# First attention: more of the softmax weights turned by DMA and VectorE, fewer by TensorE, with new step orders

## The chip, the core and the metric

The kernel runs on one core of a Trainium2 chip. The metric is the device time in microseconds (us) of one execution, lower is better. The engines are TensorE (PE, with its weight loads as PEld), VectorE (DVE), ScalarE (ACT), GpSimd (POOL) and SyncE (SP, which here only issues DMAs).

## What is computed

Two layers, each an attention onto a context and a feed-forward part, on x of shape (4, 256, 512) and a context of shape (4, 1601, 512), all in fp32. The change is in the first attention alone:

```python
# latents = layernorm(x): (4, 256, 512); context: (4, 1601, 512)
N_HEADS, N_KV_HEADS, HEAD_DIM = 32, 4, 128
hidden = concatenate([context, latents], axis=1)              # 1857 keys a batch
q = (latents @ Wq).reshape(b, 256, 4, 8, 128)
k = (hidden @ Wk).reshape(b, 1857, 4, 128)
v = (hidden @ Wv).reshape(b, 1857, 4, 128)
scores = einsum('bqhgd,bkhd->bhgqk', q, k) / sqrt(128)
attn = softmax(scores, axis=-1)
out = einsum('bhgqk,bkhd->bqhgd', attn, v).reshape(b, 256, 4096)
x = x + out @ Wo
...
```

The rest (a gated expert block, a second attention and a routed expert block) is untouched.

## The kernel before

`grouped_attention_block` first projects queries, keys and values (`split_projections`), which go to DRAM as pairs of fp32r numbers, a high and a low part. Each product of two such pairs is three matmuls, high by high, high by low, low by high (`three`). Then come 128 units, one for each of 4 batches and 32 heads; a unit has 256 tokens as two tiles j = 0, 1 of 128 rows (`QT` = 2).

For a unit and a tile j, TensorE makes the scores of 128 tokens by 1857 keys in four PSUM banks `ps_s`: half 0 is banks 0 and 1 (1024 keys), half 1 is banks 2 and 3 (833 keys), with a call of `scores(u, j, half)` each. VectorE takes the maximum of each half (`maximum`) and the negated, scaled maximum of the row (`negate_maximum`). ScalarE takes the exponential of each half into `probs` (`exponentials`), with its sum read by a second small instruction. The four banks are all there are: `scores(u, j, half)` waits until the exponential of the same half of the tile before it is done.

For the product with v the weights must be transposed, keys on the partitions. Two ways are in use:

- The first 1024 keys (`TURNED`, four runs of `RUN` = 256) are *traded*: for each tile SP issues four DMAs (`trade`), each moving one run of all 128 rows of `probs` onto 32 partitions of `traded`, which lies in the idle tile `xn`. Then VectorE's 32x32 transpose (`turn_traded`, line 898) gives a pair of key blocks for all 256 tokens in `turned`, ScalarE copies it to fp32r (`turned_high`, line 836), GpSimd subtracts to get the low part (`low`, line 707), and TensorE weighs it with v (`weigh_turned`, six matmuls of 256 columns). Four such pairs a unit, in rings of four.
- The last 833 keys are transposed by TensorE (`turn_plain`, line 752, fourteen transposes a unit into `ps_x`), copied by ScalarE (`plain_high`, line 845), subtracted by VectorE (`plain_low`, line 908) and weighed (`weigh_plain`): four pairs, of which the last has one tile of 65 keys.

All engines run over the units in steps (`run`), each engine with its own `step`, in which the calls for several units are written out by hand in the order in which the engine issues them: u, v, w, l, z are the units r, r-1, r-2, r-3, r-4. Nothing else sets the order; engines meet at semaphores (`probs_done`, `neg_max_done`, `turn_done`, `t_hi_done`, `t_done`, `x_hi_done`, `x_done` and so on), and a wait stands in the queue of its engine ahead of what follows it. SP's queue holds the trades, the loads of the next keys, values (`piece`) and queries, and the stores of the outputs (`store_output`, after VectorE's `take_output`).

After the units, `output_projection_block` multiplies with Wo.

Of the kernel before, what the change touches and what calls it, by code (L numbers as in the profile page):

```python
# [6 lines left out]
F32 = mybir.dt.float32  # L7
# [4 lines left out]
P = 128  # L12
# [476 lines left out]
def grouped_attention_block(nc, held, x, ctx_in, wq, wk, wv, wo, x_res, xn, stats, ident, ones):  # L489
# [21 lines left out]
    RUN = 256  # L511
# [5 lines left out]
    PPAIRS = -(-PLAIN // 2)  # L517
    BLOCKS = TBLOCKS + PLAIN
    plain_rows = lambda m: P if m < PLAIN - 1 else REST
    pair_tiles = lambda e: range(2 * e, min(2 * e + 2, PLAIN))  # L520
    RING, PRING, XBANKS = 4, 4, 2
    KPIECES = 4
    VPLAIN = (PLAIN - 1) // 2
# [3 lines left out]
    assert QT == 2 and len(CHUNKS) == 4 and HPG == 8 and TURNED <= 2 * BANK and TBLOCKS % 2 == 0 and WIDTH % 2 == 0  # L527
    assert PLAIN % 2 == 1 and TPAIRS * HEADS % RING == 0 and PPAIRS * HEADS % XBANKS == 0 and PPAIRS * HEADS % PRING == 0

    with ExitStack() as ctx:  # L530
# [16 lines left out]
        with ExitStack() as stack:  # L547
# [12 lines left out]
            def load_values(sp, b, g, a, c):  # L560
# [4 lines left out]
                elif c < RUNS + 2:  # L565
                    lo, hi = [(0, VPLAIN), (VPLAIN, PLAIN - 1)][c - RUNS]
                    sp.dma_start(v_buf[a][:, TBLOCKS + lo:TBLOCKS + hi, :].bitcast(F32),
                                 keys_of[TURNED + P * lo:TURNED + P * hi, g, :].rearrange("(m i) d -> i m d", i=P)
                                 ).then_inc(v_loaded[a], 16)
                else:  # L570
                    sp.dma_start(v_buf[a][0:REST, BLOCKS - 1, :].bitcast(F32), keys_of[KEYS - REST:KEYS, g, :]).then_inc(v_loaded[a], 16)
# [17 lines left out]
            traded = xn[:, :, :].rearrange("p t d -> p (t d)")[:, 0:2 * QT * TURNED].rearrange("p (a j g r) -> p a j g r", a=2, j=QT, g=RUNS)  # L589
            turned = sb("turned", [P, RING, 2, TOK])  # L590
            t_hi, t_lo = sb("t_hi", [P, RING, 2, TOK], F32R), sb("t_lo", [P, RING, 2, TOK], F32R)
            x_hi, x_lo = sb("x_hi", [P, PRING, 2, TOK], F32R), sb("x_lo", [P, PRING, 2, TOK], F32R)
# [45 lines left out]
            def _(sp):  # L638
                def trade(u, j):
                    if not u.live:  # L640
                        return
                    sp.wait_ge(probs_done, 4 * u.n + 2 * j + 1)
                    if j == 0:
                        wait(sp, turn_done, TPAIRS * (u.n - 1))
                    for c in range(RUNS):
                        sp.dma_start(traded[SQ * c:SQ * (c + 1), u.a, j, :, :], probs[j][u.a][:, RUN * c:RUN * (c + 1)]
                                     ).then_inc(trade_done[j][u.a], 16)
# [11 lines left out]
                def piece(u):  # L659
# [7 lines left out]
                    else:  # L667
                        if i == KPIECES:
                            wait(sp, tv_ps, TPAIRS * (u.n - KPIECES - HPG))
                            wait(sp, xv_ps, PPAIRS * (u.n - KPIECES - HPG))  # L670
# [31 lines left out]
            def _(pool):  # L702
                def low(u, p):
                    if u.live:
                        slot = (TPAIRS * u.r + p) % RING
                        pool.wait_ge(t_hi_done, TPAIRS * u.n + p + 1)
                        pool.tensor_tensor(t_lo[:, slot, :, :], turned[:, slot, :, :], t_hi[:, slot, :, :].bitcast(F32), ALU.subtract  # L707
                                           ).then_inc(t_done, 1)
# [11 lines left out]
            def _(pe):  # L720
# [20 lines left out]
                def turn_plain(u, e):  # L741
                    if not u.live:
                        return
                    bank = (PPAIRS * u.r + e) % XBANKS
                    if e == 0:
                        pe.wait_ge(probs_done, 4 * (u.n + 1))
                    wait(pe, x_done, PPAIRS * u.n + e + 1 - XBANKS)
                    for m in pair_tiles(e):
                        rows, c0 = plain_rows(m), TURNED + P * m
                        for j in range(QT):  # L750
                            col = TOK * (m % 2) + P * j
                            tr = pe.transpose(ps_x[0:rows, bank, col:col + P], probs[j][u.a][:, c0:c0 + rows], turn[:, :])  # L752
                    tr.then_inc(x_ps, 1)

                def output_free(u):
# [1556 lines left out]
```

## Time and profile before

| | |
|---|---|
| median of 2 runs | 3322.86 us |
| lowest, highest | 3320.5, 3325.22 us |
| span of the profiled execution | 3324.5 us, between the two runs, so that nothing stands beside the span |
| PE, DVE, ACT, POOL busy | 3185.9 (96%), 2156.2 (65%), 1702.5 (51%), 872.7 (26%) us |
| first attention's units | from some 540 to 2119 us |
| DMA queue of SP | 51.1% of 16 engines' span, 449.22 MB |

A busy share is the union of an engine's instructions over the span. Matmuls are pipelined, and their shown durations overlap, so their pace is read from one start to the next. Times in rows are us unless marked ns. In rows by order of time the first number is the start, the second the duration, and "x4" says that four instructions in a row were merged; what stands in brackets at the end is the idle time ahead and what ended it.

### The profile page before, as it was taken

The numbers are of one execution on the slowest core, as the hardware profiler recorded it, in microseconds if no ns is written. First come the engines' busy times: TensorE is split into PE (matmuls) and PEld (weight loads), VectorE is DVE, ScalarE is ACT, GpSimd is POOL, SyncE is SP. The second block draws the span as 40 slices with busy tenths as digits, with TensorE's granted clock in tenths as the row PEclk, the third lists the DMA queues.
The fourth block names the chain that finished last, engine by engine and source line by source line (L and its number), as shares of the span: only waits on it lengthen the run. The fifth ranks groups of instructions, "written<-read, shape, count | busy, mean of one in ns | idle before, by whom it ended". The sixth has DMA issues, their size and how long they took to land. (4 is left out here: it accounts for less than half of the span.)

```text
span 3324.5 us, 55156 instructions
## 1 busy us (share of the span) xinstructions
PE 3185.9 (96%) x18912; PEld 2815.0 (85%) x18912; DVE 2156.2 (65%) x3275; ACT 1702.5 (51%) x3206; POOL 872.7 (26%) x703
## 2 busy tenths in 40 slices
PE   8999998999999999999999999898988989889999
PEld 8898886999999998999989999786778878868887
DVE  4333334888888887888878888544555667745555
ACT  3332344666666666667666666323425445532222
POOL 0000121444444443444444444321003223400000
PEclk9999998999999999999999999999998999989999
DMA  7665785777766766776667775574201101111111
GB/s 251 217 210 193 241 269 167 160 161 163 164 159 161 160 160 152 162 159 160 159 153 161 160 161 125 161 238 164 73 31 38 30 26 36 39 39 47 46 39 44
DMA packets 360308, 452.24 MB, mean 136 GB/s; under 512 B 32316, under 2 KB 289644, under 8 KB 360072
## 3 DMA queue, kind: packets, MB, share of 16 engines
q1 hardware_dynamic: 360072, 449.22, 51.1%
q8 instruction: 133, 2.18, 0.3%
q14 instruction: 103, 0.84, 0.1%
HBM read 201.45 MB, written 113.43 MB: 95 GB/s over the span
## 5 line engine op out<-in xcount | busy, mean ns | idle before, releaser
L707 POOL TENSOR_TENSOR a_t_lo<-a_turned,a_t_hi 128x512 fp32r<-128x512 f32 x512 | 649.8, 1291 | 939.8 <-ACT a_t_hi L836 939.8
L827 ACT ACTIVATE a_probs<-a_ps_s,a_neg_max 128x1024 f32<-128x1024 f32 (+1 forms) x512 | 529.5, 1034 | 476.0 <-DVE a_neg_max L879 470.1
L872 DVE TENSOR_REDUCE a_half_max<-a_ps_s 128x1 f32<-128x1024 f32 (+1 forms) x512 | 571.2, 1116 | 189.5 <-PE a_ps_s L724 185.3
L722 PE MATMUL a_ps_s<-a_k_buf,a_q_buf 128*128 128x512 f32 (+1 forms) x1024 | 419.7, 410 | 18.2 <-ACT a_probs L827 11.9
L723 PE MATMUL a_ps_s<-a_k_buf,a_q_buf 128*128 128x512 f32 (+1 forms) x1024 | 386.1, 377 | 0.0
L724 PE MATMUL a_ps_s<-a_k_buf,a_q_buf 128*128 128x512 f32 (+1 forms) x1024 | 385.3, 376 | 0.0
L908 DVE TENSOR_TENSOR a_x_lo<-a_ps_x,a_x_hi 128x512 fp32r<-128x512 f32 (+1 forms) x512 | 314.5, 614 | 107.8 <-ACT a_x_hi L845 107.8
L454 DVE TENSOR_TENSOR p_out<-p_ps_j,p_out 128x512 fp32r<-128x512 f32 (+3 forms) x196 | 153.0, 781 | 326.6 <-ACT p_out L383 326.6
L898 DVE STREAM_TRANSPOSE a_turned<-xn 128x512 f32<-128x512 f32 x512 | 357.8, 699 | 1.6 <-POOL a_t_lo L707 1.6
L383 ACT ACTIVATE p_out<-p_ps_j 128x512 fp32r<-128x512 f32 (+3 forms) x196 | 141.9, 724 | 339.8 <-PE p_ps_j L288 339.7
L722 PE MATMUL a_ps_o<-a_t_hi,a_v_buf 128*128 128x256 f32 x1024 | 298.8, 292 | 6.2 <-issue 3.6
L836 ACT ACTIVATE a_t_hi<-a_turned 128x512 fp32r<-128x512 f32 x512 | 298.4, 629 | 2.0 <-DVE a_turned L898 2.0
L723 PE MATMUL a_ps_o<-a_t_lo,a_v_buf 128*128 128x256 f32 x1024 | 287.5, 281 | 0.0
L724 PE MATMUL a_ps_o<-a_t_hi,a_v_buf 128*128 128x256 f32 x1024 | 287.4, 281 | 0.0
L845 ACT ACTIVATE a_x_hi<-a_ps_x 128x512 fp32r<-128x512 f32 (+1 forms) x512 | 274.5, 537 | 24.6 <-PE a_ps_x L752 13.2
L752 PE MATMUL a_ps_x<-a_turn,a_probs 128*128 128x128 f32 (+1 forms) x1792 | 279.0, 272 | 0.0
L722 PE MATMUL a_ps_o<-a_x_hi,a_v_buf 128*128 128x256 f32 (+1 forms) x896 | 262.4, 293 | 0.0
L724 PE MATMUL a_ps_o<-a_x_hi,a_v_buf 128*128 128x256 f32 (+1 forms) x896 | 251.6, 281 | 0.0
L723 PE MATMUL a_ps_o<-a_x_lo,a_v_buf 128*128 128x256 f32 (+1 forms) x896 | 251.4, 281 | 0.0
L752 PEld LDWEIGHTS a_ps_x<-a_turn,a_probs 128*128 128x128 f32 (+1 forms) x1792 | 219.1, 140 | 35.0 <-issue 0.2
L722 PEld LDWEIGHTS a_ps_s<-a_k_buf,a_q_buf 128*128 128x128 f32 x1024 | 195.0, 190 | 49.6 <-issue 11.7
L724 PEld LDWEIGHTS a_ps_s<-a_k_buf,a_q_buf 128*128 128x128 f32 x1024 | 194.5, 190 | 34.2
(319 smaller groups left out, 7389.7 us busy)
## 6 DMA issues: line engine op xcount, KB each, us to landing
xn<-a_probs SPq DMA_DIRECT2D x1024, 128.0 KB, 3.4
a_q_all<-p_out SPq DMA_DIRECT2D x64, 512.0 KB
a_q_buf<-a_q_all SPq DMA_DIRECT2D x128, 256.0 KB, 3.3
a_k_buf<-a_k_all SPq DMA_DIRECT2D x64, 464.5 KB, 4.0
a_v_all<-p_out SPq DMA_DIRECT2D x56, 512.0 KB
a_k_all<-p_out SPq DMA_DIRECT2D x48, 384.0 KB
a_v_buf<-a_v_all SPq DMA_DIRECT2D x64, 256.0 KB
a_o_all<-a_o_part SPq DMA_DIRECT2D x128, 128.0 KB, 3.0
```

Source lines behind the costliest of these rows:

```text
L454: dve.tensor_tensor(job_views(n, 1)[0], ps, hi.bitcast(F32), ALU.subtract).then_inc(job_done, 1)
L707: pool.tensor_tensor(t_lo[:, slot, :, :], turned[:, slot, :, :], t_hi[:, slot, :, :].bitcast(F32), ALU.subtract).then_inc(t_done, 1)
L722: pe.matmul(o, w_hi, m_hi, start=first, stop=False)
L723: pe.matmul(o, w_hi, m_lo, start=False, stop=False)
L724: return pe.matmul(o, w_lo, m_hi, start=False, stop=last)
L752: tr = pe.transpose(ps_x[0:rows, bank, col:col + P], probs[j][u.a][:, c0:c0 + rows], turn[:, :])
L827: act.activation(probs[j][u.a][:, lo:hi], s_flat[:, lo:hi], ACT.Exp, bias=neg_max[:, j:j + 1], scale=SCALE, accum_out=half_sum[:, bass.ds( ...
L836: act.activation(t_hi[:, slot, :, :], turned[:, slot, :, :], ACT.Copy).then_inc(t_hi_done, 1)
L845: act.activation(x_hi[0:rows, slot, 0:m, :], ps_x[0:rows, bank, 0:TOK * m].rearrange("p (m n) -> p m n", m=m), ACT.Copy).then_inc(x_hi_don ...
L872: dve.reduce_max(half_max[:, half:half + 1], s_flat[:, lo:hi], AX.X).then_inc(max_done, 1)
L898: dve.transpose(turned[:, slot, :, :].rearrange("p k (q r) -> p k q r", r=SQ), traded[:, u.a, :, :, 2 * SQ * p:2 * SQ * (p + 1)].rearrange ...
L908: dve.tensor_tensor(x_lo[0:rows, slot, 0:m, :], ps_x[0:rows, bank, 0:TOK * m].rearrange("p (m n) -> p m n", m=m), x_hi[0:rows, slot, 0:m, ...
```

## The change

`RUN` goes from 256 to 448: 1792 of 1857 keys are traded, in seven pairs a unit where there were four, and each DMA of a trade moves 224 KB where it moved 128 KB. TensorE transposes the last 65 keys only, two transposes a unit; `turn_plain`, `plain_high`, `plain_low` and `weigh_plain` are called once a unit. `traded` gets a tile of its own beside `xn` for odd units. `turned` keeps its ring of four pairs; `t_hi` and `t_lo` get seven places. `trade` waits for the first half of the exponentials ahead of runs 0 and 1 and for the second ahead of runs 2 and 3. Values are loaded in five pieces. The orders in the step functions are new: a step of SP stores an output between the two trades, and those of GpSimd, TensorE, ScalarE and VectorE are rewritten throughout.

```diff
-    RUN = 256
+    RUN = 448
...
-    RING, PRING, XBANKS = 4, 4, 2
+    RING, PRING, XBANKS = 4, 2, 2
+    EARLY = 3
...
-    VALUE_PIECES = [(0, 1), (2, 3), (4,), (5, 6)]
+    VALUE_PIECES = [(0,), (1,), (2,), (3, 4)]
...
-            t_hi, t_lo = sb("t_hi", [P, RING, 2, TOK], F32R), sb("t_lo", [P, RING, 2, TOK], F32R)
+            t_hi, t_lo = sb("t_hi", [P, TPAIRS, 2, TOK], F32R), sb("t_lo", [P, TPAIRS, 2, TOK], F32R)
...
                 def trade(u, j):
...
-                    sp.wait_ge(probs_done, 4 * u.n + 2 * j + 1)
...
                     for c in range(RUNS):
+                        if c % 2 == 0:
+                            sp.wait_ge(probs_done, 4 * u.n + 2 * j + c // 2 + 1)
...
                     trade(u, 0)
                     piece(Unit(b, r + HPG))
+                    store_output(Unit(b, r - 3))
                     trade(u, 1)
-                    store_output(Unit(b, r - 3))
                     queries(Unit(b, r + 2))
...
             @block.gpsimd
                 def step(b, r):
                     w, l = Unit(b, r - 2), Unit(b, r - 3)
-                    low(l, 1)
-                    low(l, 2)
-                    low(l, 3)
-                    low(w, 0)
+                    for p in range(EARLY, TPAIRS):
+                        low(l, p)
+                    for p in range(EARLY):
+                        low(w, p)
...
             @block.tensor
                 def step(b, r):
-                    weigh_turned(z, 2)
-                    weigh_plain(z, 2)
-                    turn_plain(l, 1)
-                    weigh_plain(z, 3)
+                    weigh_turned(l, 0)
                     scores(v, 0, 0)
-                    turn_plain(l, 2)
+                    weigh_turned(l, 1)
+                    weigh_plain(l)
                     scores(v, 0, 1)
-                    weigh_turned(z, 3, last=True)
-                    turn_plain(l, 3)
-                    weigh_turned(l, 0, first=True)
-                    weigh_plain(l, 0)
-                    weigh_turned(l, 1)
+                    weigh_turned(l, 2)
+                    weigh_turned(l, 3)
+                    turn_plain(w)
                     scores(v, 1, 0)
-                    turn_plain(w, 0)
+                    weigh_turned(l, 4)
                     scores(v, 1, 1)
-                    weigh_plain(l, 1)
+                    weigh_turned(l, 5)
+                    weigh_turned(l, 6)
...
             @block.scalar
                 def step(b, r):
-                    exponentials(v, 1, 0)
-                    plain_high(w, 1)
-                    exponentials(v, 1, 1)
+                    exponentials(w, 1, 0)
+                    turned_high(l, 3)
+                    exponentials(w, 1, 1)
+                    turned_high(l, 4)
+                    exponentials(v, 0, 0)
+                    turned_high(l, 5)
+                    turned_high(l, 6)
+                    exponentials(v, 0, 1)
+                    plain_high(w)
                     turned_high(w, 0)
                     turned_high(w, 1)
-                    plain_high(w, 2)
-                    exponentials(u, 0, 0)
-                    plain_high(w, 3)
-                    exponentials(u, 0, 1)
                     turned_high(w, 2)
-                    turned_high(w, 3)
-                    plain_high(v, 0)
...
             @block.vector
                 def step(b, r):
-                    plain_low(l, 1)
-                    turn_traded(l, 1)
+                    turn_traded(l, 3)
+                    turn_traded(l, 4)
                     maximum(v, 0, 0)
+                    take_output(z)
+                    turn_traded(l, 5)
                     maximum(v, 0, 1)
                     negate_maximum(v, 0)
-                    turn_traded(l, 2)
-                    take_output(z)
-                    plain_low(l, 2)
-                    turn_traded(l, 3)
+                    turn_traded(l, 6)
+                    plain_low(w)
                     maximum(v, 1, 0)
-                    plain_low(l, 3)
+                    turn_traded(w, 0)
                     maximum(v, 1, 1)
                     negate_maximum(v, 1)
-                    plain_low(w, 0)
-                    turn_traded(w, 0)
+                    turn_traded(w, 1)
+                    turn_traded(w, 2)
```

## Rows read from the trace of the kernel before

**Rows 1.** Busy time by stretch, 700 to 1700 us: PE, PEld, DVE, ACT, POOL, clock, DMA.
```profile
700.00:1700.00 1000.00, 995.32 (x6844) 917.38 (x6843) 808.59 (x1237) 686.94 (x1318) 418.75 (x330) 1.00 0.71 160
```

**Rows 2.** The tile of the maxima: count, duration (ns) least, median, most, first and last start.
```profile
L879 DVE TENSOR_SCALAR a_neg_max<-a_half_max x256: 214/214/217, 550.0 to 2098.1; 128x1 f32<-128x1 f32 x128
```

**Rows 3.** In order of time, PE, from 1000 to 1013 us.
```profile
1004.01 0.42 PE L722 MATMUL a_ps_s<-a_k_buf,a_q_buf 128*128 128x512 f32 x1
...
1005.43 0.60 PE L752 MATMUL a_ps_x<-a_turn,a_probs 128*128 128x128 f32 x4
1005.79 0.48 PE L722 MATMUL a_ps_s<-a_k_buf,a_q_buf 128*128 128x512 f32 x1
...
1007.02 0.28 PE L722 MATMUL a_ps_o<-a_t_hi,a_v_buf 128*128 128x256 f32 x1
...
1007.74 0.38 PE L752 MATMUL a_ps_x<-a_turn,a_probs 128*65 128x128 f32 x2
...
1010.13 0.50 PE L722 MATMUL a_ps_s<-a_k_buf,a_q_buf 128*128 128x512 f32 x1
```

**Rows 4.** In order of time, DVE, from 1000 to 1026 us.
```profile
1001.27 1.03 DVE L872 TENSOR_REDUCE a_half_max<-a_ps_s 128x1 f32<-128x833 f32 x1
1002.33 0.21 DVE L879 TENSOR_SCALAR a_neg_max<-a_half_max 128x1 f32<-128x1 f32 x1
...
1005.17 0.70 DVE L898 STREAM_TRANSPOSE a_turned<-xn 128x512 f32<-128x512 f32 x1
1005.79 1.19 DVE L872 TENSOR_REDUCE a_half_max<-a_ps_s 128x1 f32<-128x1024 f32 x1
1007.22 1.03 DVE L872 TENSOR_REDUCE a_half_max<-a_ps_s 128x1 f32<-128x833 f32 x1 [0.24 <-PE a_ps_s L724]
1008.37 0.21 DVE L879 TENSOR_SCALAR a_neg_max<-a_half_max 128x1 f32<-128x1 f32 x1
1008.50 0.70 DVE L898 STREAM_TRANSPOSE a_turned<-xn 128x512 f32<-128x512 f32 x1
```

**Rows 5.** In order of time, ACT, from 1000 to 1026 us.
```profile
1002.67 1.12 ACT L827 ACTIVATE a_probs<-a_ps_s,a_neg_max 128x1024 f32<-128x1024 f32 x1 [1.88 <-DVE a_neg_max L879]
...
1008.87 1.11 ACT L827 ACTIVATE a_probs<-a_ps_s,a_neg_max 128x1024 f32<-128x1024 f32 x1 [1.85 <-DVE a_neg_max L879]
1009.88 0.19 ACT L827 ACTIVATION_READ_ACCUMULATOR a_probs<-a_ps_s,a_neg_max  x1
1009.98 0.37 ACT L845 ACTIVATE a_x_hi<-a_ps_x 65x256 fp32r<-65x256 f32 x1
1010.24 0.95 ACT L827 ACTIVATE a_probs<-a_ps_s,a_neg_max 128x833 f32<-128x833 f32 x1
...
1011.17 1.15 ACT L836 ACTIVATE a_t_hi<-a_turned 128x512 fp32r<-128x512 f32 x2
1012.33 0.60 ACT L845 ACTIVATE a_x_hi<-a_ps_x 128x512 fp32r<-128x512 f32 x1
```

**Rows 6.** Groups by line and shape, 700 to 1700 us: busy us, mean ns, idle before.
```profile
L707 POOL TENSOR_TENSOR a_t_lo<-a_turned,a_t_hi 128x512 fp32r<-128x512 f32 x330 | 418.9, 1291 | 579.8 <-ACT a_t_hi L836 579.8
...
L908 DVE TENSOR_TENSOR a_x_lo<-a_ps_x,a_x_hi 65x256 fp32r<-65x256 f32 x83 | 34.0, 410 | 0.0
```

**Rows 7.** DMA issues on the page: count, KB each, median us from issue to landing.
```profile
xn<-a_probs SPq DMA_DIRECT2D x1024, 128.0 KB, 3.4
```

**Rows 8.** PE in order of time, at the stage's start and its end.
```profile
551.48 0.51 PE L722 MATMUL a_ps_s<-a_k_buf,a_q_buf 128*128 128x512 f32 x1 [2.60 <-ACT a_probs L827]
...
2103.18 0.36 PE L722 MATMUL a_ps_o<-a_t_hi,a_v_buf 128*128 128x256 f32 x1 [1.74 <-POOL a_t_lo L707]
```

**Rows 9.** Busy time by stretch, as in the first group, at the same two places.
```profile
545.00:550.00 5.00, 3.87 (x11) 2.86 (x10) 2.28 (x3) 0.24 (x1) 0.00 (x0) 0.66 0.02 5
...
2102.00:2104.00 2.00, 0.82 (x7) 0.85 (x8) 1.72 (x5) 1.51 (x4) 2.00 (x2) 1.00 1.07 161
```

More of the change, by code:

```diff
@@ L669, in piece @@
                             wait(sp, tv_ps, TPAIRS * (u.n - KPIECES - HPG))
-                            wait(sp, xv_ps, PPAIRS * (u.n - KPIECES - HPG))
+                            wait(sp, xv_ps, u.n - KPIECES - HPG)
                         for c in VALUE_PIECES[i - KPIECES]:
@@ L739, in scores, with turn_plain, weigh_turned @@
                     mm.then_inc(s_ps, 1)
-                def turn_plain(u, e):
+                def turn_plain(u):
                     if not u.live:
                         return
[L744 to L752, printed above, removed]
-                    tr.then_inc(x_ps, 1)
-                def output_free(u):
-                    wait(pe, copy_done, u.n - 1)
-                    if u.first_of_group:
-                        pe.wait_ge(v_loaded[u.group_a], 16 * VPIECES * (u.group_use + 1))
-                def weigh_turned(u, p, first=False, last=False):
+                    bank = u.r % XBANKS
+                    pe.wait_ge(probs_done, 4 * (u.n + 1))
+                    wait(pe, x_done, u.n + 1 - XBANKS)
+                    for j in range(QT):
+                        tr = pe.transpose(ps_x[0:REST, bank, P * j:P * j + P], probs[j][u.a][:, TURNED:KEYS], turn[:, :])
+                    tr.then_inc(x_ps, 1)
+                def weigh_turned(u, p):
                     if not u.live:
                         return
-                    v, slot = v_buf[u.group_a], (TPAIRS * u.r + p) % RING
-                    if first:
-                        output_free(u)
+                    v = v_buf[u.group_a]
+                    if p == 0:
+                        wait(pe, copy_done, u.n - 1)
+                        if u.first_of_group:
+                            pe.wait_ge(v_loaded[u.group_a], 16 * VPIECES * (u.group_use + 1))
                     pe.wait_ge(t_done, TPAIRS * u.n + p + 1)
@@ L768, in weigh_turned, with weigh_plain @@
                         k = 2 * p + i
[L769 to L770 removed]
+                        mm = three(ps_o[:, u.a, 0:TOK], v[:, k, 0:HD], v[:, k, HD:2 * HD], t_hi[:, p, i, :], t_lo[:, p, i, :],
+                                   k == 0, k == TBLOCKS - 1)
                     mm.then_inc(tv_ps, 1)
[L773 removed]
+                def weigh_plain(u):
                     if not u.live:
                         return
[L776 to L784 removed]
+                    v, slot = v_buf[u.group_a], u.r % PRING
+                    pe.wait_ge(x_done, u.n + 1)
+                    three(ps_o[:, u.a, 0:TOK], v[0:REST, TBLOCKS, 0:HD], v[0:REST, TBLOCKS, HD:2 * HD], x_hi[0:REST, slot, :],
+                          x_lo[0:REST, slot, :], False, False).then_inc(xv_ps, 1)
                 def turn_sums():
@@ L824, in exponentials @@
                         wait(act, trade_done[j][u.a], TRADE * u.use)
-                        wait(act, x_ps, PPAIRS * (u.n - 1))
+                        wait(act, x_ps, u.n - 1)
                     lo, hi = HALVES[half]
```

67 lines of the change are left out of this document (21 added, 46 removed).

## The prediction

> **What bounds the kernel now.** I read the busy times by stretch first. From 700 to 1700 us, the middle of the first attention, TensorE is busy for 995 of 1000 us at a granted clock of 1.00, VectorE for 809, ScalarE for 687, GpSimd for 419, and the DMA engines for 0.71 [rows 1]. Taken alone this says: TensorE is the bound, so fewer transposes there is time won. It has to be checked against the order of the work, because the change also rewrites that order.
>
> The first and the last negated maximum stand 1548.1 us apart [rows 2], and there are 127.5 units between them: 12.14 us a unit, half a unit 6.07. I then followed one half unit in order of time, to see whether anything beside TensorE's own work closes in the same time. It does. The reader should follow the four score banks: scores(j,0) starts; 1.42 us later come four transposes (0.36), then scores(j,1) (1.23 with the switch back) [rows 3]; 0.20 after the last score the second maximum starts, 1.15 later the negation, 0.50 later the exponential [rows 4, 5], whose sum is read 1.20 after its start, and 0.06 after that the next scores(j,0) starts, since it overwrites the first two banks. Sum 6.12 us, which is just the distance of the two score starts in the rows (1004.01 to 1010.13). So today two limits meet: the loop through the score banks, and TensorE's queue, which fills the 3.1 us between scores(j,1) and the next scores(j,0) with weighing. Whatever is now put *into* that loop costs its full length; what is taken from TensorE outside of it gives nothing.
>
> **The change, part by part.** Write n for the unit whose scores are made.
>
> *TensorE's work.* Twelve of fourteen transposes a unit go: three groups of four, 0.36 us each and some 0.07 for the switch back (scores(j,1) took 1.23; its columns at the pace of scores(j,0), 1.42 for six of 512, would take 1.16) [rows 3]: 3 x 0.43 = 1.3 us. The weighing keeps its size (45 matmuls of 256 columns, 0.72 for six). TensorE alone would need 12.1 - 1.3 = 10.8 us a unit.
>
> *VectorE, ScalarE, GpSimd.* Three full subtractions (plain_low) become three more 32x32 transposes (turn_traded, one each 0.62 us [rows 4]); one subtraction of 65x256, 0.41 us, stays [rows 6]. ScalarE trades copies for copies of the same shape. GpSimd goes from four to seven subtractions of 1.29 us: 9.0 us a unit [rows 6]. None of these sums reaches 12 us, so no engine's load is the bound; the order is.
>
> *The order.* All of these queues work in the order in which the step functions issue, so I wrote out who stands in front of whom. Three places matter.
>
> (1) ScalarE: `turned_high(w, 1)` and `turned_high(w, 2)` end a step, and `exponentials(w, 1, 0)` of the next step stands behind them. VectorE makes what they read, `turn_traded(w, 1)` and `turn_traded(w, 2)`, only *after* `negate_maximum(v, 1)`. So the exponential that was ready 0.34 to 0.50 after the negation now waits for two transposes and a copy more.
>
> (2) VectorE: `plain_low(w)` stands ahead of both `maximum(v, 1, ...)`. It needs `plain_high(w)`, which on ScalarE stands behind `exponentials(v, 0, 1)` and two turned_high. So the maxima of the second half wait for nearly all of ScalarE's step.
>
> (3) TensorE: between scores(v,0,0) and scores(v,0,1) stand a weigh_turned and the plain weighing, 0.72 + 0.36, where four transposes stood.
>
> The cycle that this closes, from exponentials(n,0,0) once round to exponentials(n+1,0,0), worked out from rows already shown [rows 3 to 5]:
>
> First half: the exponential until ScalarE's next instruction 1.11 (1008.87 to 1009.98); two turned_high 1.16; exponential of 833 until the next instruction 0.93; plain_high of 65x256 0.37, and 0.06 to another engine; plain_low 0.41; first maximum 1.19; turn_traded(n-1,0) 0.62; second maximum until its negation 1.10 (1.06 and 1.15 in the rows); negation until the next transpose 0.13; two transposes 0.62 + 0.70, and 0.06; turned_high 0.58. Sum 9.04 us.
>
> Second half: exponentials(n,1,0) until its sum is read, and over to TensorE, 1.26; scores(n+1,0,0) 1.42; weigh_turned 0.72; plain weighing 0.36; scores(n+1,0,1) 1.16; to the start of the maximum 0.20; maximum 1.10; negation to exponential 0.42. Sum 6.64 us.
>
> Together 15.68 us. VectorE's rows start up to 0.08 before the one ahead has ended (1005.17 plus 0.70 against 1005.79), twice in this chain, so I take 15.5. The low end is 15.2 (both maxima at 1.06, the negation's hand-over at 0.34, the copy's overlap). For the high end, no row shows a turned_high waiting right behind its transpose or a plain_low behind so late a copy; if each of some nine crossings costs 0.12 instead of 0.06 or a little less, it is 16.2. Below 15.2 I see nothing, since each link is an instruction in a queue or a wait that the code names.
>
> Each of the queues was assumed to keep its order. The rows bear that out: VectorE, ScalarE and GpSimd never start an instruction ahead of one that stands before it in the step [rows 4, 5]. The Trainium skill says it outright, on the page "TensorE: Matmul & The Clock Gate", section "Architectural detail: the array is 16× 32×32, not 1× 128×128": only TensorE's queue may pull something forward, and then only weight loads, while ScalarE's and VectorE's are strict first-in first-out. By that rule, too, the exponential cannot pass the turned_high ahead of it.
>
> *Beside the cycle.* TensorE would work 10.8 of 15.5 us, in pieces, with gaps of up to 1.8 us (behind weigh_turned(l,6), until GpSimd has made the next unit's first pair, and again until scores). GpSimd's 9.0 us lie inside the 15.5. The ring of four turned pairs doesn't bind: turn_traded(w,2) needs low(l,5), done over 4 us before.
>
> *DMA.* A trade grows from 128 KB to 224 KB in the same number of pieces. Today a unit costs 0.71 x 12.1 = 8.6 us of all DMA engines [rows 1], for 1.9 MB, of which the eight trades are 1.05 MB. If a piece costs the same whatever its length it stays 8.6; if by bytes, 8.6 + 0.75 x 4.7 = 12.1 us. Both are under 15.5. Latency: the last trade of a unit's second half is issued about 4 us after its exponential starts and lands 3.4 us after that [rows 7], or 6 us if it grows with the bytes, thus at 7.4 to 10; turn_traded(w,0) wants it at 6.6 + 5.2 = 11.8. Hidden, by 2 us at least. SP's two waits instead of one per trade and the moved store_output hold up only SP, whose eight trades of 0.6 us each leave it idle for over half of the unit.
>
> *The sum.* 127.5 x (15.5 - 12.14) = 428 us. Start-up and tail stay: their first units run on the score loop alone, as now, and the last unit has three more pairs to go through GpSimd, 4 us. The profiled execution spans 3324.5 us, 1.6 us off the median 3322.9. So 3324.5 + 428 = about 3750 us; by the ends of the cycle 3715 and 3842.
>
> **The rivals.** *Faster: TensorE stays the bound.* If ScalarE did not stand still at the end of its step, and the weighing filled each gap, a unit would take 10.8 us: 3324.5 - 127.5 x 1.3 = 3158 us. For it: TensorE's 995 of 1000 us. Against it: the two named waits lie in program order, and the score loop alone, with 1.08 and 0.72 us put between its halves, is longer than 10.8. It decides the other way only if turn_traded(w,1) and (w,2) were ready before the negation, which VectorE's order excludes. Chance 0.06.
>
> *Only the score loop grows.* If places (1) and (2) were covered, what is left is 6.64 plus a second half of 6.64 - 0.36 = 6.28: 12.9 us a unit, 3421 us (12.6 us, 3383, with the shorter hand-overs). Chance 0.06.
>
> *TensorE's clock falls.* With gaps, the granted clock can drop to the lower of its two levels. In the start of this stage it was 0.66 where gaps of 2.6 us lay between the bursts; near its end it stayed at 1.00 with a gap of 1.74 us and TensorE busy 0.82 of 2 us [rows 8, 9]. My longest gap is 1.8, so I expect 1.00. At the lower level throughout, TensorE's links in the cycle (1.42 + 0.72 + 0.36 + 1.16 = 3.66 us) double: 3750 + 467 = 4217, but its whole work would then be 21 us a unit, without the gaps that brought the clock down, so about half the time at most: some 3985 us. [...] Chance 0.08.
>
> **How the numbers follow.** The cycle as worked out: 0.80, with 3750 us. Its ends are 3715 and 3842; with start-up and tail uncertain by some ten us I give 3700 to 3850. The other cases, 0.20 together, stay outside. About 2% (66 us) is what a measurement of this kernel can tell from no change: faster 0.06; within 2% 0.03, half of the second rival; slower 0.91.
>
> **What would show it.** Units of about 15.5 us between negated maxima; TensorE busy about 0.7 in the stage, at a clock of 1.00; VectorE idle some 3 us a unit ahead of plain_low, waiting for ScalarE's x_hi; ScalarE waiting for VectorE's turned at the end of its step, and no longer for the negated maximum ahead of half of its exponentials; TensorE waiting for the exponentials. It would be wrong if the exponentials of the second half still start 0.4 us after their negation, if VectorE waits for traded data ahead of turn_traded(w,0), or if the clock is under 1.

## The result, and the profile after

The changed kernel took 3909.4 us (median of two runs, 3908.3 and 3910.5), against 3322.9 before: a ratio of 1.177, with an interval of 1.174 to 1.179. It is slower, as forecast, but the time lies above the range of 3700 to 3850. The page of the changed kernel: its span, the busy time of each engine, the granted clock and the DMA share in 40 slices, and the two kinds of trade (count, KB each, us from issue to landing):

```profile
span 3908.7 us, 53700 instructions
...
PE 3268.7 (84%) x17376; PEld 2806.6 (72%) x17376; DVE 2146.6 (55%) x3275; ACT 1707.4 (44%) x3206; POOL 1348.7 (35%) x1087
...
PEclk9999989999998999899898989988989899999999
DMA  7665979999999999999999999997741111111111
...
xn<-a_probs SPq DMA_DIRECT2D x512, 224.0 KB, 5.9
a_traded<-a_probs SPq DMA_DIRECT2D x512, 224.0 KB, 5.9
```

The tile of the negated maxima, which answers to [rows 2]:

```profile
L855 DVE TENSOR_SCALAR a_neg_max<-a_half_max x256: 212/214/216, 550.5 to 2681.4; 128x1 f32<-128x1 f32 x128
```

2681.4 - 550.5 is 2130.9 us, over 127.5 units 16.71 us a unit, where it was 12.14. The difference, 4.57 us, times 127.5 is 583 us; the spans differ by 3908.7 - 3324.5 = 584. So all of the loss lies inside the stage, as 4.57 us a unit on average; start and tail did not move.

Busy time by stretch (PE, PEld, DVE, ACT, POOL, granted clock, DMA share, GB/s), first the middle of the stage, which answers to [rows 1], then stretches that are read below:

```profile
700.00:2400.00 1700.00, 1290.06 (x7195) 1121.20 (x7194) 987.22 (x1523) 849.22 (x1623) 892.54 (x711) 0.91 1.04 162
...
1262.00:1264.00 2.00, 0.86 (x4) 0.60 (x3) 0.60 (x2) 2.00 (x5) 2.00 (x2) 0.64 1.00 245
1264.00:1266.00 2.00, 2.00 (x6) 1.55 (x5) 0.00 (x0) 1.23 (x3) 2.00 (x3) 0.50 1.00 221
1266.00:1268.00 2.00, 2.00 (x11) 1.96 (x10) 1.73 (x3) 0.00 (x0) 0.64 (x1) 0.50 1.07 154
1268.00:1270.00 2.00, 2.00 (x10) 1.71 (x10) 0.50 (x2) 0.00 (x0) 0.00 (x0) 0.65 1.06 153
...
1236.00:1262.00 26.00, 19.23 (x124) 16.88 (x123) 16.67 (x27) 13.50 (x26) 12.98 (x11) 1.00 1.04 162
```

No engine is full any more: TensorE is busy 0.76 of the stage instead of 0.995, VectorE 0.58, GpSimd 0.53, ScalarE 0.50. Two columns are not as forecast: the clock is 0.91, and the DMA share is 1.04 (the share adds up the time of all packets, so packets that overlap can bring it over 1). Who waits for whom, in the same stretch (engine, line, waited for: us in total, times, longest):

```profile
POOL a_t_lo L701 <- ACT a_t_hi L815: 807.5, 309, 6.8
DVE a_half_max L848 <- PE a_ps_s L718: 376.0, 177, 3.7
ACT a_t_hi L815 <- DVE a_turned L874: 351.8, 204, 2.7
DVE a_x_lo L882 <- ACT a_x_hi L822: 305.6, 101, 3.4
ACT a_probs L806 <- DVE a_neg_max L855: 288.3, 61, 6.2
...
PE a_ps_s L716 <- ACT a_probs L806: 237.3, 203, 1.8
...
DVE a_turned L874 <- DMA xn<-a_probs: 0.3, 1, 0.3
```

Some 102 units lie in these 1700 us. VectorE's plain_low (a_x_lo) waits 101 times for ScalarE's copy, about 3 us each: place (2) of the prediction. ScalarE's turned_high waits 204 times, twice a unit, for VectorE's transposes. In the unit shown next the first of the two waits, 2.32 us, is for `turn_traded(w, 0)`, which VectorE makes between the two maxima that place (2) holds up; the second, 1.15 us, is the one of place (1). Only one wait for traded data is there, of 0.3 us.

ScalarE in order of time (start, us, instruction, and in brackets the idle time ahead of it and what ended it), which answers to [rows 5]; one unit, then the three exponentials that bound the halves of a later one:

```profile
1204.28 1.11 ACT L806 ACTIVATE a_probs<-a_ps_s,a_neg_max 128x1024 f32<-128x1024 f32 x1 [5.15 <-PE a_ps_x L742]
...
1207.35 0.37 ACT L822 ACTIVATE a_x_hi<-a_ps_x 65x256 fp32r<-65x256 f32 x1
1210.04 0.63 ACT L815 ACTIVATE a_t_hi<-a_turned 128x512 fp32r<-128x512 f32 x1 [2.32 <-DVE a_turned L874]
1211.82 1.23 ACT L815 ACTIVATE a_t_hi<-a_turned 128x512 fp32r<-128x512 f32 x2 [1.15 <-DVE a_turned L874]
1212.95 1.09 ACT L806 ACTIVATE a_probs<-a_ps_s,a_neg_max 128x1024 f32<-128x1024 f32 x1
...
1221.13 1.11 ACT L806 ACTIVATE a_probs<-a_ps_s,a_neg_max 128x1024 f32<-128x1024 f32 x1 [5.02 <-DVE a_neg_max L855]
...
1238.09 1.11 ACT L806 ACTIVATE a_probs<-a_ps_s,a_neg_max 128x1024 f32<-128x1024 f32 x1 [5.14 <-PE a_ps_x L742]
...
1246.76 1.10 ACT L806 ACTIVATE a_probs<-a_ps_s,a_neg_max 128x1024 f32<-128x1024 f32 x1
...
1253.40 1.11 ACT L806 ACTIVATE a_probs<-a_ps_s,a_neg_max 128x1024 f32<-128x1024 f32 x1 [3.48 <-DVE a_neg_max L855]
```

VectorE in the first of these units, which answers to [rows 4]:

```profile
1207.76 0.42 DVE L882 TENSOR_TENSOR a_x_lo<-a_ps_x,a_x_hi 65x256 fp32r<-65x256 f32 x1 [3.12 <-ACT a_x_hi L822]
1208.10 1.21 DVE L848 TENSOR_REDUCE a_half_max<-a_ps_s 128x1 f32<-128x1024 f32 x1
...
1210.87 0.21 DVE L855 TENSOR_SCALAR a_neg_max<-a_half_max 128x1 f32<-128x1 f32 x1
1211.00 2.48 DVE L874 STREAM_TRANSPOSE a_turned<-a_traded 128x512 f32<-128x512 f32 x4
```

The negated maximum of the second half is there at 1211.08. Its exponential starts at 1212.95, behind two copies that wait for the transposes that VectorE begins at 1211.00. Ahead of that, the maximum at 1208.10 stands behind plain_low, which has stood still for 3.12 us. From exponential to exponential, the first half is 1212.95 - 1204.28 = 8.67 us (worked out: 9.04), the second 1221.13 - 1212.95 = 8.18 (worked out: 6.64). In the later unit, from 1238.09 to 1253.40, the first half takes 8.67 us again and the second 6.64, just as worked out.

So the excess is in the second half, that of TensorE's links, and only in some units. TensorE in order of time, two units, of which the first is the later one of ScalarE's rows; the scores of a unit begin at 1239.35, 1254.66 and 1272.84:

```profile
1239.35 0.50 PE L716 MATMUL a_ps_s<-a_k_buf,a_q_buf 128*128 128x512 f32 x1 [1.29 <-ACT a_probs L806]
...
1245.88 0.38 PE L716 MATMUL a_ps_o<-a_t_hi,a_v_buf 128*128 128x256 f32 x1 [1.58 <-POOL a_t_lo L701]
...
1248.00 0.50 PE L716 MATMUL a_ps_s<-a_k_buf,a_q_buf 128*128 128x512 f32 x1 [1.16 <-ACT a_probs L806]
...
1254.66 0.50 PE L716 MATMUL a_ps_s<-a_k_buf,a_q_buf 128*128 128x512 f32 x1 [1.15 <-ACT a_probs L806]
1255.00 0.40 PE L717 MATMUL a_ps_s<-a_k_buf,a_q_buf 128*128 128x512 f32 x1
1255.24 0.40 PE L718 MATMUL a_ps_s<-a_k_buf,a_q_buf 128*128 128x512 f32 x1
...
1261.19 0.39 PE L716 MATMUL a_ps_o<-a_t_hi,a_v_buf 128*128 128x256 f32 x1 [1.59 <-POOL a_t_lo L701]
...
1263.31 0.80 PE L716 MATMUL a_ps_s<-a_k_buf,a_q_buf 128*128 128x512 f32 x1 [1.14 <-ACT a_probs L806]
1263.90 0.63 PE L717 MATMUL a_ps_s<-a_k_buf,a_q_buf 128*128 128x512 f32 x1
1264.33 0.63 PE L718 MATMUL a_ps_s<-a_k_buf,a_q_buf 128*128 128x512 f32 x1
...
1272.84 0.50 PE L716 MATMUL a_ps_s<-a_k_buf,a_q_buf 128*128 128x512 f32 x1 [1.28 <-ACT a_probs L806]
```

The first unit is 15.31 us long and runs wholly at a clock of 1.00 (the stretch from 1236 to 1262 above). The second is 18.18 us long: from 1263.31 on its scores follow each other every 0.43 us, where those from 1255.00 took 0.24, while the clock is 0.50 from 1264 to 1268 and 0.64 and 0.65 in the stretches beside them: some 7 us at the low level, worked out from these four shares. The longest gap of either unit is 1.59 us. At the mean of 16.71, the clock costs 16.71 - 15.31 = 1.40 us a unit, 178 us in all, if 15.31 stands for every unit at full clock; the first experiment tests that.

### The profile page after: what moved, and what is told of

The parts are those of the page before. It is cut to its first block and busy times, and to the rows that moved or that the text cites. A ratio compares the mean times of both kernels' runs of the same rounds, so it can differ in the third digit from the quotient of the medians.

```text
span 3908.7 us, 53700 instructions
## 1 busy us (share of the span) xinstructions
PE 3268.7 (84%) x17376; PEld 2806.6 (72%) x17376; DVE 2146.6 (55%) x3275; ACT 1707.4 (44%) x3206; POOL 1348.7 (35%) x1087
## 5 line engine op out<-in xcount | busy, mean ns | idle before, releaser
L701 POOL TENSOR_TENSOR a_t_lo<-a_turned,a_t_hi 128x512 fp32r<-128x512 f32 x896 | 1126.2, 1281 | 1051.0 <-ACT a_t_hi L815 1051.0
L815 ACT ACTIVATE a_t_hi<-a_turned 128x512 fp32r<-128x512 f32 x896 | 542.3, 625 | 448.8 <-DVE a_turned L874 448.8
L716 PE MATMUL a_ps_o<-a_t_hi,a_v_buf 128*128 128x256 f32 x1792 | 542.4, 303 | 217.2 <-POOL a_t_lo L701 204.8
L716 PE MATMUL a_ps_s<-a_k_buf,a_q_buf 128*128 128x512 f32 (+1 forms) x1024 | 452.2, 442 | 306.7 <-ACT a_probs L806 300.8
L716 PEld LDWEIGHTS a_ps_o<-a_t_hi,a_v_buf 128*128 128x128 f32 x1792 | 366.0, 204 | 260.6 <-POOL a_t_lo L701 177.0
L717 PE MATMUL a_ps_o<-a_t_lo,a_v_buf 128*128 128x256 f32 x1792 | 526.5, 294 | 0.0
L718 PE MATMUL a_ps_o<-a_t_hi,a_v_buf 128*128 128x256 f32 x1792 | 523.4, 292 | 0.0
L716 PEld LDWEIGHTS a_ps_s<-a_k_buf,a_q_buf 128*128 128x128 f32 x1024 | 215.1, 210 | 391.4 <-ACT a_probs L806 313.9
L718 PE MATMUL a_ps_s<-a_k_buf,a_q_buf 128*128 128x512 f32 (+1 forms) x1024 | 432.5, 422 | 0.0
L717 PE MATMUL a_ps_s<-a_k_buf,a_q_buf 128*128 128x512 f32 (+1 forms) x1024 | 428.7, 419 | 0.0
L717 PEld LDWEIGHTS a_ps_o<-a_t_lo,a_v_buf 128*128 128x128 f32 x1792 | 365.0, 204 | 16.3
L718 PEld LDWEIGHTS a_ps_o<-a_t_hi,a_v_buf 128*128 128x128 f32 x1792 | 361.8, 202 | 0.0
L874 DVE STREAM_TRANSPOSE a_turned<-a_traded 128x512 f32<-128x512 f32 x448 | 293.3, 687 | 18.2 <-issue 13.7
L874 DVE STREAM_TRANSPOSE a_turned<-xn 128x512 f32<-128x512 f32 x448 | 293.3, 687 | 1.1 <-POOL a_t_lo L701 0.5
L718 PEld LDWEIGHTS a_ps_s<-a_k_buf,a_q_buf 128*128 128x128 f32 x1024 | 219.9, 215 | 43.4
L717 PEld LDWEIGHTS a_ps_s<-a_k_buf,a_q_buf 128*128 128x128 f32 x1024 | 218.3, 213 | 28.3
```

What stands on the lines that cost most here:

```text
L701: pool.tensor_tensor(t_lo[:, p, :, :], turned[:, slot, :, :], t_hi[:, p, :, :].bitcast(F32), ALU.subtract).then_inc(t_done, 1)
L716: pe.matmul(o, w_hi, m_hi, start=first, stop=False)
L717: pe.matmul(o, w_hi, m_lo, start=False, stop=False)
L718: return pe.matmul(o, w_lo, m_hi, start=False, stop=last)
L815: act.activation(t_hi[:, p, :, :], turned[:, slot, :, :], ACT.Copy).then_inc(t_hi_done, 1)
L874: dve.transpose(turned[:, slot, :, :].rearrange("p k (q r) -> p k q r", r=SQ), traded[u.a][:, :, :, 2 * SQ * p:2 * SQ * (p + 1)].rearrange ...
```

## The experiments

Theory A: the order of the queues makes the cycle of 15.3 us, and the low clock of TensorE adds 1.4 us. The rivals: B, the DMA engines, whose share reads 1.04, make the rest (or all) of it; C, the sum of 15.5 was right by accident, and moving the two places gives nothing. Times below are medians; the time of a unit, the clock, the share, GB/s and the rows are of the one profiled execution, which lies up to 29 us from its median.

**TensorE kept busy.** Fourteen matmuls a unit that nobody reads are put where it waits; nothing is taken away:

```diff
+                def fill(count, bank):
+                    for _ in range(count):
+                        pe.matmul(ps_x[:, bank, TOK:TOK + P], turn[:, :], turn[:, :], start=True, stop=True)
...
+                    fill(6, r % XBANKS)
                     weigh_turned(l, 0)
+                    fill(4, r % XBANKS)
                     scores(v, 0, 0)
...
                     turn_plain(w)
+                    fill(4, (r + 1) % XBANKS)
                     scores(v, 1, 0)
```

> The changed kernel with 14 matmuls of 128x128 a unit added on TensorE, in the three places where it stands still (ahead of the first weighing pair, ahead of scores(v,0,0), ahead of scores(v,1,0)); they write a free part of a ps_x bank that nobody reads, so the output is the same. Theory: the cycle of queue orders is 15.3 us a unit at a clock of 1.00 (1239.35 to 1254.66 in the changed kernel's trace), and the clock, 0.90 in the stage, adds the other 1.4 us. Then the added work lifts the clock to 1.00 and the kernel gets FASTER: 3324.5 + 127.5 x (15.3 - 12.14) = 3727 us, 3710 to 3760. Rival, DMA sets the pace (share 1.04): no change, 3909. Rival, the gaps are not what lowers the clock: 3909 or more, up to 14 x 0.2 us x 128 = 358 us more if the added matmuls lie on the path.

Measured: 3765.0 us, 1.134 times before (1.132 to 1.136), so 144 us faster than the changed kernel with more work, and 5 us above the range that was expected. The negated maxima run from 555.1 to 2527.4: 15.47 us a unit. The stage as a stretch:

```profile
700.00:2300.00 1600.00, 1503.34 (x10217) 1363.90 (x10218) 1003.99 (x1548) 865.93 (x1656) 913.00 (x725) 1.00 1.07 176
```

And TensorE in order of time:

```profile
1202.61 0.39 PE L716 MATMUL a_ps_o<-a_t_hi,a_v_buf 128*128 128x256 f32 x1 [0.26 <-POOL a_t_lo L701]
...
1204.73 0.50 PE L716 MATMUL a_ps_s<-a_k_buf,a_q_buf 128*128 128x512 f32 x1 [0.25 <-ACT a_probs L813]
```

Where gaps of 1.58 and 1.16 us lay, 0.26 and 0.25 are left, the clock is 1.00 throughout, and the unit has the forecast length. The trades are as large as in the changed kernel, at a share of 1.07. The clock was the excess.

**Half of each trade.** From the third unit on, only half of each run is moved, so that half of the turned weights are stale:

```diff
-                        sp.dma_start(traded[u.a][SQ * c:SQ * (c + 1), j, :, :], probs[j][u.a][:, RUN * c:RUN * (c + 1)]
+                        m = RUN if u.n < 2 else RUN // 2
+                        sp.dma_start(traded[u.a][SQ * c:SQ * (c + 1), j, :, 0:m], probs[j][u.a][:, RUN * c:RUN * c + m]
```

> The changed kernel, but from the third unit on each trade moves only the first half of each run, 112 KB instead of 224; the other half of the traded tile keeps old weights, so the attention is computed from partly stale weights. Same number of DMAs, same semaphores. Theory (order of the queues and the clock): no change, 3909 within 1%, landing times fall from 5.9 us. Rival, DMA sets the pace: a unit's 2.7 MB falls to 1.8 MB, the period from 16.7 to some 12 to 15 us, so 3300 to 3700 us.

Measured: 3898.4 us, 1.173 (1.171 to 1.175): 0.3% off the changed kernel, 16.66 us a unit, the clock still at 0.91:

```profile
700.00:2300.00 1600.00, 1217.12 (x6789) 1058.44 (x6790) 930.92 (x1437) 801.30 (x1533) 842.30 (x671) 0.91 0.38 108
```

A trade lands after 2.7 us instead of 5.9, the share falls from 1.04 to 0.38, and the time stays. With the single wait of 0.3 us above, rival B is out for the changed kernel: its transfers are hidden.

**Place (1) undone.** On ScalarE the copies of pairs 1 and 2 move behind the exponential that they stood ahead of:

```diff
                     exponentials(w, 1, 0)
-                    turned_high(l, 3)
+                    turned_high(l, 1)
                     exponentials(w, 1, 1)
+                    turned_high(l, 2)
+                    turned_high(l, 3)
                     turned_high(l, 4)
...
                     turned_high(w, 0)
-                    turned_high(w, 1)
-                    turned_high(w, 2)
```

> The changed kernel with ScalarE's order alone changed: turned_high(w,1) and (w,2) no longer stand ahead of the next exponentials(w,1,0), but behind it. Theory: two transposes, a copy and their hand-overs (2.5 us) leave the cycle for a hand-over of 0.42, and weigh_turned(l,1) comes 0.4 later: 15.3 - 1.7 = 13.6 to 14.4 us a unit at full clock, 3510 to 3613 us; if the clock falls as often as now, up to 3790. Rival, DMA sets the pace: 3909.

Measured: 3682.7 us, 1.108 (1.104 to 1.113), 14.85 us a unit. ScalarE in order of time:

```profile
1203.72 1.11 ACT L806 ACTIVATE a_probs<-a_ps_s,a_neg_max 128x1024 f32<-128x1024 f32 x1 [2.94 <-DVE a_neg_max L855]
...
1209.71 0.63 ACT L815 ACTIVATE a_t_hi<-a_turned 128x512 fp32r<-128x512 f32 x1 [2.54 <-DVE a_turned L874]
1210.88 1.11 ACT L806 ACTIVATE a_probs<-a_ps_s,a_neg_max 128x1024 f32<-128x1024 f32 x1 [0.54 <-DVE a_neg_max L855]
```

The exponential now waits for its negation alone, and the first half is 7.16 us instead of 8.67. The time lies above the range expected at full clock (3510 to 3613) and inside the one with the clock still falling: it was 0.96 from 700 to 2300 us. Rival C is out.

**Places (1) and (2) undone,** with whole and with half trades. On VectorE `plain_low(w)` moves behind the negated maximum and `turn_traded(w, 1)`; the fifth kernel has the half trades of the second one as well:

```diff
                     turn_traded(l, 6)
-                    plain_low(w)
                     maximum(v, 1, 0)
...
                     turn_traded(w, 1)
+                    plain_low(w)
                     turn_traded(w, 2)
```

> As the run before it, and on VectorE plain_low(w) is moved from ahead of the maxima of the second half to behind the negation and one transpose. Theory: both detours are out, the score loop and the 0.4 of weigh_turned(l,1) are left: 6.28 + 7.05 = 13.3 us a unit, 12.6 if the loop's hand-overs are short, 3385 to 3480 us, clock near 1.00. Rival, DMA sets the pace at 16.7 us: 3909, with VectorE's turn_traded waiting for the traded tile.

> The kernel with ScalarE's and VectorE's detours both taken out, with half the bytes in each trade from the third unit on (so partly stale weights). It measured 14.7 us a unit with full trades where 12.6 to 13.3 was worked out. If the trades' bytes are the difference: 12.6 to 13.5 us a unit, 3385 to 3500 us, clock 1.00, no wait for a traded tile. If something in the queues was overlooked: 3640 as before.

Measured: 3640.9 us, 1.096 (1.092 to 1.099), 14.69 us a unit with whole trades, hardly better than place (1) alone and a miss, since 3385 to 3480 us was expected; with half trades 3494.4 us, 1.051 (1.049 to 1.053), 13.50 a unit. The stage with whole trades:

```profile
700.00:2300.00 1600.00, 1274.47 (x7675) 1108.66 (x7673) 1062.21 (x1623) 897.15 (x1732) 961.03 (x757) 0.96 1.07 184
```

And with half trades:

```profile
700.00:2000.00 1300.00, 1099.59 (x6827) 948.21 (x6826) 945.91 (x1442) 798.43 (x1539) 856.30 (x674) 0.99 0.47 133
```

Here the size of a trade matters, by 1.2 us a unit, where it was worth 0.05 in the changed kernel. The first of the two has waits for traded data (46.3 us in 29 waits for one buffer, 18.5 in 16 for the other, in 1300 us), the second has none. These waits come to 0.7 of the 1.2 us; how much of the rest is the clock, 0.96 against 0.99, was not separated. The bound that places (1) and (2) had hidden is the next one: the trades. Place (2) was undone only together with place (1), and place (3) only in the rewrite that follows, so neither has a price of its own.

**The score loop freed of everything.** All step orders are rewritten so that both halves of the scores stand next to each other and the weighing fills the wait for the exponentials. The new orders, with the loops written out (GpSimd, left out here, now takes four pairs early instead of three):

```diff
# TensorE
+ scores(v, 0, 0); scores(v, 0, 1)
+ weigh_plain(z); weigh_turned(z, 4); weigh_turned(z, 5); weigh_turned(z, 6); turn_plain(w)
+ scores(v, 1, 0); scores(v, 1, 1)
+ weigh_turned(l, 0); weigh_turned(l, 1); weigh_turned(l, 2); weigh_turned(l, 3)
# ScalarE
+ exponentials(v, 0, 0); exponentials(v, 0, 1); turned_high(l, 4); turned_high(l, 5); turned_high(l, 6); plain_high(w)
+ exponentials(v, 1, 0); exponentials(v, 1, 1); turned_high(w, 0); turned_high(w, 1); turned_high(w, 2); turned_high(w, 3)
# VectorE
+ maximum(v, 0, 0); maximum(v, 0, 1); negate_maximum(v, 0)
+ turn_traded(l, 4); turn_traded(l, 5); turn_traded(l, 6); take_output(z); plain_low(l)
+ maximum(v, 1, 0); maximum(v, 1, 1); negate_maximum(v, 1)
+ turn_traded(w, 0); turn_traded(w, 1); turn_traded(w, 2); turn_traded(w, 3)
```

> All step orders written anew around the score loop, with the 448 runs kept: TensorE makes both halves of a tile's scores one behind the other and weighs in the gap behind them (four pairs, then three and the plain block); ScalarE and VectorE do the copies and transposes in the gap behind each tile's exponentials and negation; the plain subtraction comes a step later. If only the order matters, a half unit is 1.26 + 1.42 + 1.16 + 0.20 + 1.10 + 0.42 = 5.56 us: 11.2 us a unit, 3205 us. What the order of two rows back showed speaks for a second limit: there VectorE waited for traded tiles, at 14.7 us a unit and a DMA share of 1.07. If the trades cannot go faster than that, this run is no faster: 14.7 us, 3650 us.

And the same with half trades, half of the turned weights stale:

> The kernel with both halves of the scores together, but from the third unit on each trade moves the first half of each run only (112 KB), so the attention uses partly stale weights. Theory (order gives 11.2 us a unit as soon as the trades are out of the way): 3180 to 3240 us. Rival (it is not the trades' bytes that hold the run with full trades): the same time as that run.

Measured: with whole trades 3412.8 us, 1.027 (1.021 to 1.032), 12.71 us a unit, between the 3205 and the 3650 us of the two cases expected; with half trades 3211.5 us, 0.966 (0.964 to 0.968), 11.23 a unit. Waits in the first of them, 700 to 2000 us:

```profile
PE a_ps_s L716 <- DMA a_q_buf<-a_q_all: 101.2, 63, 4.8
...
DVE a_turned L869 <- DMA xn<-a_probs: 68.6, 38, 4.6
DVE a_turned L869 <- DMA a_traded<-a_probs: 42.0, 31, 4.4
```

Its stage as a stretch:

```profile
700.00:2000.00 1300.00, 1169.94 (x7264) 1043.60 (x7263) 992.63 (x1536) 852.67 (x1640) 901.98 (x716) 0.96 1.07 214
```

And that of the one with half trades, which has no wait for a transfer:

```profile
700.00:2000.00 1300.00, 1272.72 (x8211) 1149.31 (x8210) 1120.06 (x1736) 947.02 (x1850) 1028.03 (x815) 0.99 0.57 157
```

The order takes 4.0 us off a unit, with the same transfers, what the clock gave back (0.96 for 0.91) included. Free of them, a unit is shorter than the 12.14 us before. A better order alone could hardly do that, since TensorE was busy for 995 of 1000 us before [rows 1]: it takes the change's smaller work on TensorE. (The kernel before was not run in this order.) But 3211 us is no version, since it moves half of what must be moved. What stays between 11.23 and 12.71 goes with waits for transfers, among them TensorE's for the queries that stand behind the trades in SP's queue (landing 10.5 us against 3.2 with half trades), and with a clock of 0.96 for 0.99.

**Five attempts on the transfers,** all on that order and with whole data. The odd runs issued from ScalarE's queue instead of SP's:

> The kernel with both halves of the scores together, full trades, but runs 1 and 3 of each trade are issued from ScalarE's queue, behind its copies, and runs 0 and 2 from SyncE's. A run lands on 32 of the 128 partitions; with one queue all 16 DMA engines write to the same 32 at a time, with two queues to 64. If that is what holds the trades near 184 GB/s, the rate rises and a unit takes 11.2 to 13 us, 3205 to 3440 us. If the limit is the DMA engines' own or the reading side, no change against the run with one queue.

The queries issued ahead of the second trade of a unit instead of behind it:

> The kernel with both halves of the scores together (12.7 us a unit, 3413 us), and SyncE issues the next queries ahead of the second trade of a unit instead of behind it. There TensorE waited 101 us in 1300 for the queries, which landed 10.5 us after their issue. If that wait was worth its length: 0.08 x 12.7 = 1.0 us a unit, 3285 us. If the DMA engines as a whole are at their limit, the wait moves to VectorE's turn_traded: 3413 as before.

The same, with each run landing as two pieces of 224 weights:

> As the run with the early queries, but every run is laid down in two rows of 224 weights with 32 unused places between, so that a trade of the same 224 KB goes in 256 pieces of 896 bytes instead of 128 of 1792, in the same number of DMAs (the inverse sums share the tile of the sums, to make room). With half runs the pieces of 896 bytes cost so little that the DMA share fell from 1.04 to 0.38 while the bytes fell by a third only. If it is the length of a piece that is dear: share 0.9 or less, 11.2 to 11.6 us a unit, 3200 to 3260 us. If bytes count, or the partitions that a trade writes to: no change against the run with the early queries.

That one with the odd runs from ScalarE's queue:

> As the run with split pieces, and runs 1 and 3 of each trade are issued from ScalarE's queue. With whole pieces two queues gave 3366 against 3413 us, 1.4%. If the limit is where the pieces land, the two changes add: 3200 us; if the split has already taken the trades out of the way, it is the same or a little slower than the split alone, by ScalarE's issues.

Queries early and runs of 384 instead of 448, 192 KB a DMA, with three tiles left to TensorE's transposes:

> A version between the two: runs of 384, so 1536 keys are traded (192 KB a DMA, 2.4 MB a unit instead of 2.7) and 321 keys, in two pairs, are transposed by TensorE; the step orders are those with both halves of the scores together, queries ahead of the second trade. TensorE's work is 10.45 us for the matmuls and 0.43 + 0.2 for six transposes and their switches, some 11.2 us; the score loop 11.2; the trades at the 214 GB/s of the runs of 448 with this order would take 11.4. Theory: 11.3 to 11.7 us a unit, 3220 to 3270 us, faster than both kernels by 1.5 to 3% over the one before. If the trades are held by something that full use of the DMA engines brings with it whatever the bytes, 12 us or more: 3310 or slower.

Measured (us, ratio to before with its interval, us a unit, then clock, share and GB/s from 700 to 2000 us; the profiled execution with early queries took 3385.6 us, 29 above its median, so its last four numbers are those of an unusually long one):

| kernel | us | ratio | a unit | clock | share | GB/s |
|---|---|---|---|---|---|---|
| two queues | 3365.9 | 1.013 (1.010 to 1.015) | 12.46 | 0.98 | 1.07 | 219 |
| queries early | 3356.2 | 1.009 (1.007 to 1.011) | 12.61 | 0.96 | 1.06 | 215 |
| split pieces | 3385.2 | 1.020 (1.017 to 1.022) | 12.48 | 0.98 | 1.11 | 219 |
| split, two queues | 3357.8 | 1.008 (1.005 to 1.011) | 12.36 | 0.97 | 1.10 | 221 |
| runs of 384 | 3388.0 | 1.021 (1.019 to 1.023) | 12.60 | 0.97 | 1.06 | 195 |

Against 3412.8, two queues give 1.4% and early queries 1.7%; all three together give no more than early queries alone. The 3366 us of two queues lie in the wide range that was expected if the landing place holds the trades, but the rate went only from 214 to 219 GB/s, so this decides nothing. Early queries were to give 3285 us, or 3413 if the wait only moved; much of it moved: in 1300 us TensorE's wait for queries is gone, and VectorE's for traded data went from 110.6 to 168.1 us. Split pieces were to give 3200 to 3260 us and came out 0.9% slower than early queries alone, so cutting the pieces shorter does not help. The last one is a clear miss: from fewer bytes I had worked out 3220 to 3270 us, and it came to 3388. VectorE's largest wait for a transfer in it:

```profile
DVE a_turned L897 <- DMA xn<-a_probs: 125.2, 45, 6.1
```

A trade of 192 KB still took 7.2 us to land (7.4 and 7.7 with 224 KB in the first version of this order). So the time isn't simply one of bytes either. Part of this miss is not the trades': TensorE also waited 84.0 us in 47 waits for plain_low ahead of its transposes, in the same 1300 us. What holds the trades back (their landing on 32 partitions each, the queue, or the loads beside them) stays open; where a run lands was not varied. No version with whole data beat the kernel before.

## Why the prediction was off

The order of the queues was right, in place and in size. At full clock a unit takes 15.31 us in the trace and 15.47 with the filler, where 15.5 (15.2 to 16.2) was worked out; the filled kernel's 3765 us lies 15 us from the forecast. Each wait that was to show it is there: plain_low 3.12 us behind ScalarE's copy, the copies of pairs 1 and 2 behind VectorE, the exponential behind them and not behind its negation, TensorE busy 0.74 of the stretch at full clock. Undoing place (1) gave 1.86 us a unit (1.51 of it in the half that it stands in), undoing both with the transfers made small 3.2, what the clock gave back included. The first half took 8.67 us for 9.04, so the sum of 15.68 was 0.37 too long there; the second took the 6.64 us worked out wherever the clock was 1.00.

**The step that failed** is the rival "TensorE's clock falls": "My longest gap is 1.8, so I expect 1.00", with a chance of 0.08. The gap was even shorter, 1.59 us, and the clock still fell to 0.50. The reason rested on one place near the stage's end, where a gap of 1.74 us had left it at 1.00 [rows 8, 9] (the same trace has one more there, of 1.63 us, 5 us later, also at 1.00). Here a unit has three gaps, 1.58, 1.16 and 1.15 us in the first one shown, unit after unit, and for that case no row of before stood. That the clock might be under 1 was named among the signs of being wrong, but the 0.08 gave it next to no weight. The price was cut wrongly as well: I worked it out for the low clock throughout and for half of the time, 3985 us, as if it were a yes or a no. It came as some 7 us of low clock in the unit of 18.18 us shown, as none in the one before it, and 1.40 us a unit on average, 0.38 of the 3.66 us of TensorE's links. 3324.5 + 127.5 x (15.31 - 12.14) = 3729, plus the 178 us of the clock, makes 3907; the profiled execution took 3910.5. With the filler a unit is 16.71 - 15.47 = 1.24 us shorter, 158 us in all (144 by the medians); the 0.16 us a unit that are left of the 1.40 are at most what its own matmuls cost.

The Trainium skill has the warning, on the page "TensorE: Matmul & The Clock Gate", section "A second HAM failure mode: psum-queue depth-cycling", a section that I passed over: a kernel that cycles through PSUM banks leaves TensorE idle for short times between groups, often enough that its clock swings between the two levels. This trace agrees: two of a unit's three gaps end when score banks come free, and the stage's clock is 0.91.

**DMA** was hidden, as said, but its size was missed. The share was to be 8.6 to 12.1 of 15.5 us, 0.56 to 0.78; it was 1.04 of 16.71, 17.4 us, with landing at 5.9 us, the 6 that I gave as the upper case. The higher estimate gave the trades' bytes the mean price of all transfers of the stage; with 112, 128 and 224 KB a DMA of a trade, a unit's share comes to 0.38 x 16.66 = 6.3, 8.6 and 17.4 us, so it grew faster than the bytes. It cost next to nothing in this kernel (0.05 us a unit), and became the next limit in both better orders in which the trades were halved as well.

**The other rivals.** "TensorE stays the bound" (10.8 us a unit) did not come about with the order as written; with the score loop freed and the transfers made small it is 11.23 at TensorE busy for 1272.7 of 1300 us, so the work that the change takes off TensorE is real. "Only the score loop grows" (12.6 to 12.9) is what undoing both places leaves if transfers are no bound: 13.50 measured, 0.6 over its price.

## What to carry to other kernels

When in-order queues share a buffer that goes round a loop (here the four score banks), write down for every engine what stands ahead of the instructions of that loop; put the work that the loop does not need behind them: here what stood inside it was paid for although no engine was busy for more than 0.76 of the stage. Do not treat the clock as a yes or no by the longest gap: if a change turns a full TensorE into one with several short gaps a unit, price a share of low clock on its links. And test what a relieved bound uncovers: halving the trades was worth 0.3% in the changed kernel, 4% with the two places undone and 6% with the loop freed.

## What the runs showed of the hardware

- TensorE, busy 0.76 of the stage with no gap over 1.6 us in the units shown, ran at 0.50 for some 7 us in one of the two units shown, and at 0.91 on the whole; matmuls that compute nothing, put into the gaps, brought the stage back to 1.00 and saved 144 us. Two units with nearly the same gaps ran one at 1.00 and the next partly at 0.50, so the gaps' lengths alone do not tell which unit is hit.
- The DMA share is no measure of what is left. It read 1.04 at 162 GB/s with next to no wait, and 1.06 to 1.11 at 214 to 221 GB/s in other orders with the same data; halving the bytes of each trade, with the same number of DMAs, took it from 1.04 to 0.38, while the rate fell by a third only.
